# Local attention: the scores of even and odd heads on eight small tiles of TensorE and in two PSUM banks, the turned weights in the bank of the turned queries and keys

## The chip, the cores and the metric

One core of a Trainium2 chip runs the whole program. The metric is the time of one execution on the device, in microseconds; three runs of the kernel before are shown, and one more execution was profiled. PE is TensorE, ACT ScalarE, DVE VectorE, POOL GpSimd, SP SyncE.

## What is computed

The input x is [8, 512, 128]. After a layer norm, two branches are added to it: a causal attention (16 heads of 8) and a six-layer local transformer with 16 heads of 64 and windows of 32 tokens. The change is in the local attention of the six layers, cut here to what matters (`look` puts the window before in front of each window, so that 32 queries see 64 keys):

```python
x = attn_layer(shift_tokens(x), Wqkv[i], q_scale[i], k_scale[i], Wo[i]) + x      # six times, each with an ffn_layer after it
q, k, v = split(x @ Wqkv)                       # 16 heads of 64
q, k = l2norm(q) * qs, l2norm(k) * ksc          # then rotated by position
bq = q.reshape(b, h, nw, 32, 64); bk2, bv2 = look(k), look(v)     # [b, h, nw, 64, 64]
sim = einsum('bhwie,bhwje->bhwij', bq, bk2) * 8
attn = softmax(where(mask, -max, sim), -1)
out = einsum('bhwij,bhwje->bhwie', attn, bv2) @ Wo
```

All of it is float32.

## The kernel before, in words

**Work and order.** The tokens of a layer are 32 tiles of 128 (8 batches of 4). `pipeline` (L240) is a software pipeline over tiles that PE, ACT, DVE and POOL each write out by hand in the same `step`: step t handles tile t with lag 0, the tile before it with lag 1, and so on up to lag 6. A step has a first half (`wp` = 0) and a second half (`wp` = 1). The engines run their instructions strictly in the order written and meet only through semaphores. The first 6 steps of a layer fill the pipeline, the middle ones are a loop of four steps a pass, the last ones drain it. The six layers are 192 tiles.

**A tile's way.** The 1024 queries and 1024 keys of a token come in four chunks `c` of 512 (0 and 1 are the queries, 2 and 3 the keys).
- PE `project(c)` (L587) writes chunk c into one of two banks with three matmuls of 512 columns.
- ACT `square(c)` (L933) squares it. DVE `rotate(c)` (L1227, the multiplication at L1236) multiplies it by the rotation and frees the bank. POOL `add(c)` (L1505) adds the halves.
- DVE sums the squares (L1246), ACT `norms` (L949, L952, L956) makes of them the inverse norms `rn`, POOL `scale` (L1519) multiplies the chunk by them.
- A tile later, PE `turn_qk(c)` (L602, transposes at L614) turns the chunk in four transposes into `rbank`, the one bank for this, and ACT `turned_qk(c)` (L959) copies it out: chunks 0 and 1 with two copies of 64 partitions each into `qbd`, chunks 2 and 3 with one into `kT`. The semaphore `ev` counts these copies, and the next `turn_qk` waits for it, because it writes the same bank. `windows` (PE L665, transposes at L673, ACT L1012, semaphore `xwev`) uses `rbank` too, once a step, between chunks 2 and 3.
- Two tiles later, PE `score(wp)` (L618) adds the scores of two of the four windows of a tile to a mask that ACT `mask_ahead` (L985) copied into `sbank` beforehand. `qbd` holds the queries of two heads in the two diagonal blocks of a 128 x 64 operand, the rest is zero: 16 matmuls of 128 rows, 64 columns and 64 moving columns give 8 pairs of heads for two windows. Each float32 matmul shows as two matmuls and two weight loads in the profile.
- DVE `shift(wp)` (L1249) takes the maximum of each row (L1256) and subtracts it (L1259, semaphore `sub`), ACT `exp` (L983), DVE `sums` (L1269, L1271), POOL `normalise` (L1527, semaphore `pn`).
- PE `turn_p(wp)` (L637, transposes at L645) turns the weights into a bank of their own, `tbank`. ACT `turned_p` (L993) copies them out into `pT` (semaphore `ptev`). PE `weigh` (L649) multiplies them with the tokens of the windows, ACT `weighed` (L1002) copies the result into `ysb`.
- PE `project_out` (L677) multiplies four of the 16 heads by `wvo` in each half of most steps; DVE adds the sum to x.

**The order of one step.** On PE, in each half: turn_qk(2wp), project(2wp), project(2wp+1), turn_p(wp), in the second half windows, then weigh, score(wp), turn_qk(2wp+1), project_out (L702 to L712). On ACT, in each half: mask_ahead, turned_qk(2wp), square(2wp), square(2wp+1), exp, norms, in the second half windows, then turned_p, weighed, in the first half heads_of_tokens, and turned_qk(2wp+1) (L1022 to L1035). On DVE: rotate, rotate, sums, shift, square_sums (L1300 to L1305). On POOL: add(2wp), in the second half load_next (L1475, L1477), scale, scale, normalise, add(2wp+1), in the first half rests_of_tile (L1484) (L1531 to L1540).

All matmuls are recorded at L401, all plain copies of ACT at L790.

## Time and profile before

| | |
|---|---|
| runs | 3914.37, 3914.64, 3911.06 us; median 3914.37 us |
| the profiled execution | 3916.98 us |
| its span, from the first to the last instruction | 3915.2 us |
| its mean granted TensorE clock | 0.960 |
| busy: PE, ACT, DVE, POOL | 3617.0, 3010.4, 2778.3, 2730.6 us |

How it is read: by busy time PE leads, with 92% of the span, before ACT (77%), DVE (71%) and POOL (70%). A matmul's end is modelled in the profile, so starts are read for PE rather than ends. The time between two starts on one engine is what an instruction costs it; where an instruction starts a few hundredths of a microsecond after another engine's instruction has ended, it waited for that.

### The profile page before, as it was taken

The numbers are of one execution on the slowest core, as the hardware profiler recorded it, in microseconds if no ns is written. First come the engines' busy times: TensorE is split into PE (matmuls) and PEld (weight loads), VectorE is DVE, ScalarE is ACT, GpSimd is POOL, SyncE is SP. The second block draws the span as 40 slices with busy tenths as digits, with TensorE's granted clock in tenths as the row PEclk, the third lists the DMA queues.
The fourth block names the chain that finished last, engine by engine and source line by source line (L and its number), as shares of the span: only waits on it lengthen the run. The fifth ranks groups of instructions, "written<-read, shape, count | busy, mean of one in ns | idle before, by whom it ended". The sixth has DMA issues, their size and how long they took to land.

```text
span 3915.2 us, 94663 instructions
## 1 busy us (share of the span) xinstructions
PE 3617.0 (92%) x30894; PEld 2685.2 (69%) x30894; DVE 2778.3 (71%) x3770; ACT 3010.4 (77%) x6096; POOL 2730.6 (70%) x2889
## 2 busy tenths in 40 slices
PE   6898689999889999899999899999799999799998
PEld 3444367777667777677777677777577776577776
DVE  4566377776677776677776677776677776677776
ACT  3555478888688887688887688886688886788885
POOL 3454378886388884588884688883688882788872
PEclk7999789999999999899999899999899999899999
DMA  4223200000100000000001000001000001000002
GB/s 132 85 90 92 56 1 1 0 0 1 30 2 1 0 0 22 9 2 0 0 0 29 2 2 0 0 0 29 2 2 0 0 0 29 2 1 0 0 1 71
DMA packets 59745, 67.76 MB, mean 17 GB/s; under 512 B 12006, under 2 KB 40164, under 8 KB 58468
## 3 DMA queue, kind: packets, MB, share of 16 engines
q1 hardware_dynamic: 59492, 64.64, 5.8%
q8 instruction: 128, 2.10, 0.2%
q14 instruction: 125, 1.02, 0.1%
HBM read 46.27 MB, written 18.35 MB: 17 GB/s over the span
## 4 chain that ended last, share of the span: by engine, by line
POOL 41%; issue 29%; PE 19%; ACT 5%; DVE 3%; POOLq 2%; DMA 1%; SPq 1%; ACTq 0%; DVEq 0%
PE bank L401 16%; POOL sb_area L1505 16%; POOL sb_area L1519 12%; POOL sb_area L1527 6%; POOL sb_xs L1477 2%; POOL sb_xs L1475 2%; POOL sb_xwin L1484 2%; PE bank L614 2%; ACT sb_area L790 1%; DVE sb_area L1157 1%; ACT sb_area L940 1%; ACT sb_area L983 1%; DMA sb_wqk_lo<-qk_rows 1%; ACT sb_area L842 0%; ACT sb_lnb L952 0%
## 5 line engine op out<-in xcount | busy, mean ns | idle before, releaser
L790 ACT ACTIVATE sb_area<-bank 128x512 f32<-128x512 f32 (+4 forms) x2149 | 1315.2, 648 | 266.2 <-PE bank L614 206.4
L1236 DVE TENSOR_TENSOR sb_area<-bank,sb_rots 128x1024 f32<-128x1024 f32 x768 | 907.4, 1220 | 625.6 <-ACT sb_area L940 619.0
L1505 POOL TENSOR_TENSOR sb_area<-sb_area 128x512 f32<-128x512 f32 x768 | 983.6, 1281 | 311.8 <-DVE sb_area L1236 311.3
L401 PE MATMUL bank<-sb_area 128*64 128x64 f32 (+6 forms) x17104 | 1053.9, 276 | 10.2 <-DMA sb_area<-in_c_crot 3.5
L401 PEld LDWEIGHTS bank<-sb_area 128*64 128x64 f32 (+4 forms) x17104 | 750.0, 146 | 280.8 <-issue 244.0
L1519 POOL TENSOR_TENSOR sb_area<-sb_area,sb_rn 128x512 f32<-128x512 f32 x768 | 785.0, 1043 | 49.9 <-POOL sb_xs L1477 40.8
L401 PE MATMUL bank<-sb_area,sb_wvo 128*128 128x256 f32 x3072 | 728.3, 381 | 3.1 <-DVE sb_xT L1291 3.1
L401 PE MATMUL bank<-sb_wqk_hi,sb_xwin 128*128 128x512 f32 x1536 | 606.6, 436 | 43.0 <-POOL sb_xwin L1484 38.4
L614 PE MATMUL bank<-sb_ident,sb_area 128*128 128x128 f32 x3072 | 507.3, 288 | 134.1 <-POOL sb_area L1519 90.0
L401 PEld LDWEIGHTS bank<-sb_area,sb_wvo 128*128 128x128 f32 x3072 | 555.0, 190 | 75.2 <-issue 8.8
L614 PEld LDWEIGHTS bank<-sb_ident,sb_area 128*128 128x128 f32 x3072 | 330.9, 143 | 304.4 <-POOL sb_area L1519 211.7
L940 ACT ACTIVATE sb_area<-bank 128x512 f32<-128x512 f32 x768 | 439.2, 597 | 82.8 <-PE bank L401 42.7
L1246 DVE TENSOR_REDUCE sb_ssq<-sb_area 128x16 f32<-128x1024 f32 x384 | 464.1, 1209 | 0.0
L1527 POOL TENSOR_TENSOR sb_area<-sb_area,sb_srec 128x512 f32<-128x512 f32 x384 | 401.2, 1045 | 81.1 <-DVE sb_srec L1271 81.1
L401 PE MATMUL bank<-sb_wqk_lo,sb_xwin 128*128 128x512 f32 (+4 forms) x1280 | 423.0, 414 | 29.7 <-POOL sb_xwin L1412 13.8
L401 PEld LDWEIGHTS bank<-sb_wqk_hi,sb_xwin 128*128 128x128 f32 x1536 | 303.3, 197 | 109.0 <-issue 43.4
L790 ACT ACTIVATE bank<-sb_lmask 128x512 f32<-128x512 bf16 x384 | 231.0, 601 | 100.7 <-DVE sb_area L1259 95.1
L1269 DVE TENSOR_REDUCE sb_ssum<-sb_area 128x8 f32<-128x512 f32 x384 | 260.0, 677 | 45.6 <-ACT sb_area L983 45.6
L1259 DVE TENSOR_TENSOR sb_area<-bank,sb_smax 128x512 f32<-128x512 f32 x384 | 265.6, 692 | 13.1
L1256 DVE TENSOR_REDUCE sb_smax<-bank 128x8 f32<-128x512 f32 x384 | 253.0, 659 | 24.8 <-PE bank L401 24.5
L401 PEld LDWEIGHTS bank<-sb_wqk_lo,sb_xwin 128*128 128x128 f32 (+1 forms) x1280 | 206.4, 200 | 88.5 <-issue 26.8
L1157 DVE TENSOR_REDUCE sb_area<-bank 128x2 f32<-128x1024 f32 (+3 forms) x256 | 203.6, 823 | 88.6 <-PE bank L401 87.1
(116 smaller groups left out, 4107.3 us busy)
## 6 DMA issues: line engine op xcount, KB each, us to landing
qk_rows<-sb_p SPq DMA_DIRECT2D x52, 256.0 KB, 4.2
sb_wqk_hi<-qk_rows SPq DMA_DIRECT2D x32, 256.0 KB, 2.9
sb_wqk_lo<-qk_rows SPq DMA_DIRECT2D x32, 256.0 KB, 2.7
sb_area<-in_Wqkv SPq DMA_DIRECT2D x7, 1024.0 KB, 5.7
sb_area<-in_WvT SPq DMA_DIRECT2D x7, 512.0 KB, 7.5
sb_wo_bd<-in_Wo SPq DMA_DIRECT2D x14, 256.0 KB, 8.5
sb_area<-in_x SPq DMA_DIRECT2D x4, 512.0 KB, 6.0
sb_area<-in_x SPq DMA_DIRECT2D x8, 256.0 KB, 2.9
```

The lines of the kernel that those rows point to most:

```text
L401: return nc.tensor.matmul(o, a, b, start=start, stop=stop, skip_group_check=True)
L614: m = nc.tensor.transpose(rbank[:, j * P:(j + 1) * P], qn[:, c, j * P:(j + 1) * P], ident[:, :])
L790: return nc.scalar.activation(o, i, ACT.Copy)
L940: nc.scalar.activation(sqb[:, c, :], pj[c % 2][:, :], ACT.Square).then_inc(S["sq"], 1)
L1236: tt_(t12[:, c % 2, :, :].rearrange("p u (h d) -> p u h d", h=8), src, bc(rots[:, tt, s, :, :], [P, 2, 8, D], 2), ALU.mult).then_inc(S["ro ...
L1246: nc.vector.tensor_reduce(ssq[:, tt % 2, half, :], sqb[:, 2 * half:2 * half + 2, :].rearrange("p c (h d) -> p (c h) d", h=8), AX.X, ALU.add)\
L1256: nc.vector.tensor_reduce(smax[:, wp, :], s3, AX.X, ALU.max).then_inc(S["smax"], 1)
L1259: tt_(dd[:, wp, :].rearrange("p (h k) -> p h k", h=HP), s3, bc(smax[:, wp, :], [P, HP, 64], 2), ALU.subtract).then_inc(S["sub"], 1)
L1269: nc.vector.tensor_reduce(ssum[:, wp, :], d3, AX.X, ALU.add).then_inc(S["ssum"], 1)
L1505: pt_(qn[:, c, :].rearrange("p (h e d) -> p h e d", h=8, e=2), t12[:, c % 2, 0, :].rearrange("p (h e d) -> p h e d", h=8, e=2), swapped, A ...
L1519: pt_(sums_of_heads, sums_of_heads, r, ALU.mult).then_inc(S["qn"], 1)
L1527: pt_(dd[:, wp, :].rearrange("p (h k) -> p h k", h=HP), dd[:, wp, :].rearrange("p (h k) -> p h k", h=HP), srec[:, wp, :].unsqueeze(2).to_b ...
```

## The change

The scores of a head go on a tile of TensorE of their own: 64 rows (even heads on partitions 0 to 63, odd heads on 64 to 127) by 32 columns (the 32 queries of a window), and the even heads' scores go to one bank, the odd ones' to another. `qbd` is read without its zero blocks. 16 matmuls of 128 rows by 64 columns become 32 of 64 rows by 32 columns, each over 64 moving columns, ordered so that eight in a row use eight different tiles. The second bank is what was `tbank`; `turn_p` now uses `rbank`, between turn_qk(2wp) or windows and turn_qk(2wp+1), with the waits that this needs. `windows` moves ahead of project(3) on PE and ahead of square(3) on ACT; on ACT `turned_p` moves ahead of `norms`. The waits of `score` become a function of their own, `masked_and_turned`, which is called before `weigh`. Masking, maximum and subtraction read or write the two banks as [128, 2, 256]. The order of heads changes with it, and `project_out` takes the blocks of `wvo` in the new order.

```diff
-        pj, rbank, sbank, tbank, ybank, mbank = ps[0:2], ps[2], ps[3], ps[4], ps[5:7], ps[7]
+        pj, rbank, ybank, mbank = ps[0:2], ps[2], ps[5:7], ps[7]
+        sbanks = banks[:, 3:5, 0:256]
...
                     # turn_qk
+                        if c % 2 == 1 and (w := behind(t, i, part, 3)):
+                            pe.wait_ge(S["ptev"], g_of(w[1]) * 8 + 2 * w[0] + c // 2 + 1)
...
-                    def score(wp):
+                    def masked_and_turned(wp):
+
                         if not (v := behind(t, i, part, 2)):
                             return
                         tt, bt = v
                         pe.wait_ge(S["ev"], g_of(bt) * 16 + 4 * tt + 4)
                         if part == 0 and t == 2 and wp == 0:
                             pe.wait_ge(S["sub"], g_of(bt) * 8)
-                            mm(sbank[:, :], identb[:, :], lmask[:, 0, :], True, False)
+                            pe.wait_ge(S["ptev"], g_of(bt) * 8)
+                            for h2 in range(2):
+                                mm(sbanks[:, h2, :], identb[:, :], lmask[:, 0, 256 * h2:256 * h2 + 256], True, False)
                         else:
                             pe.wait_ge(S["masked"], g_of(bt) * 8 + 2 * tt + wp)
-                        for g in range(HP):
-                            for x in range(2):
-                                hp, w = 2 * (g // 2) + x, wp + 2 * (g % 2)
-                                k0 = tt * P + w * WIN
-                                m = mm(sbank[64 * x:64 * x + 64, g * 64:(g + 1) * 64],
-                                       qbd[:, tt % 2, hp, w, :, :].rearrange("p a b -> p (a b)"),
-                                       kT[:, hp, k0:k0 + 2 * WIN], False, x == 1 and g == HP - 1)
+
+                    def score(wp):
+                        if not (v := behind(t, i, part, 2)):
+                            return
+                        tt, bt = v
+                        for i_ in range(2):
+                            for w in range(2):
+                                k0, c0 = tt * P + (wp + 2 * w) * WIN, (2 * i_ + w) * 64
+                                for j in range(4):
+                                    for h2 in range(2):
+                                        rows, hp = slice(64 * h2, 64 * h2 + 64), 4 * i_ + j
+                                        m = mm(sbanks[WIN * j:WIN * j + WIN, h2, c0:c0 + 64],
+                                               qbd[rows, tt % 2, hp, wp + 2 * w, h2, :], kT[rows, hp, k0:k0 + 2 * WIN],
+                                               False, i_ == 1 and w == 1)
                         m.then_inc(S["score"], 1)
...
                     # turn_p
                         pe.wait_ge(S["pn"], m_ + 2)
                         pe.wait_ge(S["ptev"], m_)
+                        if v := behind(t, i, part, 1):
+                            if wp == 0:
+                                pe.wait_ge(S["ev"], g_of(v[1]) * 16 + 4 * v[0] + 1)
+                            else:
+                                pe.wait_ge(S["xwev"], g_of(v[1]) * 4 + v[0] + 1)
+                        else:
+                            pe.wait_ge(S["ev"], (l + 1) * (16 * B))
                         for j in range(4):
-                            m = nc.tensor.transpose(tbank[:, j * P:(j + 1) * P], dd[:, wp, j * P:(j + 1) * P],
+                            m = nc.tensor.transpose(rbank[:, j * P:(j + 1) * P], dd[:, wp, j * P:(j + 1) * P],
                                                     ident[:, :])
...
                     # project_out
-                                m = mm(mbank[:, 0:256], wvo[:, h, :], ysb[:, hf, :, h * WIN:(h + 1) * WIN],
+                                m = mm(mbank[:, 0:256], wvo[:, 2 * (h % HP) + h // HP, :], ysb[:, hf, :, h * WIN:(h + 1) * WIN],
...
                         turn_qk(2 * wp)
                         project(2 * wp)
+                        if wp == 1:
+                            windows()
+                        weighing = behind(t, i, part, 4 - wp)
+                        if not weighing:
+                            masked_and_turned(wp)
                         project(2 * wp + 1)
                         turn_p(wp)
-                        if wp == 1:
-                            windows()
+                        if weighing:
+                            masked_and_turned(wp)
                         weigh(4 - wp, 1 - wp)
                         score(wp)
                         turn_qk(2 * wp + 1)
...
                     # ACT: mask_ahead, turned_p, and the order of a half
-                        copy(sbank[:, :], lmask[:, 0 if first else 1, :]).then_inc(S["masked"], 1)
+                        copy(sbanks, lmask[:, 0 if first else 1, :].rearrange("p (b n) -> p b n", b=2)).then_inc(S["masked"], 1)
...
-                        copy(pT[:, wp, :], tbank[:, :]).then_inc(S["ptev"], 1)
+                        copy(pT[:, wp, :], rbank[:, :]).then_inc(S["ptev"], 1)
...
                         square(2 * wp)
+                        if wp == 1:
+                            windows()
                         square(2 * wp + 1)
                         exp(3 - wp, 1 - wp)
+                        turned_p(wp)
                         norms(1 - wp, 1 - wp)
-                        if wp == 1:
-                            windows()
-                        turned_p(wp)
                         weighed(4 - wp, 1 - wp)
...
                     # DVE: shift
-                        s3 = sbank[:, :].rearrange("p (h k) -> p h k", h=HP)
-                        nc.vector.tensor_reduce(smax[:, wp, :], s3, AX.X, ALU.max).then_inc(S["smax"], 1)
+                        s3 = sbanks.rearrange("p b (h k) -> p b h k", h=4)
+                        nc.vector.tensor_reduce(smax[:, wp, :].rearrange("p (b h) -> p b h", b=2), s3, AX.X, ALU.max).then_inc(S["smax"], 1)
...
```

## Rows read from the trace of the kernel before

**Rows 1.** Busy time (instructions) of PE, PEld, DVE, ACT, POOL over one step.

```profile
1453.62:1468.01 14.39, 14.27 (x137) 11.07 (x135) 11.05 (x15) 12.62 (x27) 12.30 (x14) 1.00 0.00 0
```

**Rows 2.** Timeline of PE over that step: start, length in us, instructions.

```profile
1456.52 1.89 PE L401 MATMUL bank<-sb_area,sb_wvo 128*128 128x256 f32 x8
1458.48 0.65 PE L614 MATMUL bank<-sb_ident,sb_area 128*128 128x128 f32 x4
...
1460.48 0.66 PE L645 MATMUL bank<-sb_ident,sb_area 128*128 128x128 f32 x4
1461.07 2.22 PE L401 MATMUL bank<-sb_area 64*128 64x256 f32 x40
1463.21 0.66 PE L614 MATMUL bank<-sb_ident,sb_area 128*128 128x128 f32 x4
1463.71 1.89 PE L401 MATMUL bank<-sb_area,sb_wvo 128*128 128x256 f32 x8
1465.65 0.63 PE L614 MATMUL bank<-sb_ident,sb_area 128*128 128x128 f32 x4
...
1466.59 0.63 PE L401 MATMUL bank<-sb_wqk_hi,sb_xwin 128*128 128x512 f32 x2
...
1467.53 0.60 PE L645 MATMUL bank<-sb_ident,sb_area 128*128 128x128 f32 x4
1467.96 0.38 PE L673 MATMUL bank<-sb_ident,sb_xs 128*128 128x128 f32 x2
```

**Rows 3.** Timeline of ACT over that step.

```profile
1455.02 0.21 ACT L956 ACTIVATE sb_rn<-sb_lnb 128x16 f32<-128x16 f32 x1
...
1459.17 1.20 ACT L790 ACTIVATE sb_area<-bank 64x512 f32<-64x512 f32 x2 [0.81 <-PE bank L614]
1460.39 1.08 ACT L940 ACTIVATE sb_area<-bank 128x512 f32<-128x512 f32 x2
1461.36 0.63 ACT L983 ACTIVATE sb_area<-sb_area 128x512 f32<-128x512 f32 x1
...
1462.73 1.51 ACT L790 ACTIVATE sb_area<-bank 128x512 f32<-128x512 f32 x2
...
1464.32 1.19 ACT L790 ACTIVATE sb_area<-bank 64x512 f32<-64x512 f32 x2
1465.53 0.60 ACT L790 ACTIVATE bank<-sb_lmask 128x512 f32<-128x512 bf16 x1
1466.32 0.60 ACT L790 ACTIVATE sb_area<-bank 128x512 f32<-128x512 f32 x1 [0.19 <-PE bank L614]
1467.02 1.30 ACT L940 ACTIVATE sb_area<-bank 128x512 f32<-128x512 f32 x2
```

**Rows 4.** Groups by shape, whole trace: busy us, mean ns of one, idle us before.

```profile
L401 PE MATMUL bank<-sb_area,sb_wvo 128*128 128x256 f32 x3072 | 728.3, 381 | 3.1 <-DVE sb_xT L1291 3.1
...
L401 PEld LDWEIGHTS bank<-sb_area 128*64 128x64 f32 x12288 | 392.1, 138 | 125.4 <-issue 125.4
```

**Rows 5.** Timeline of DVE over that step, one row.

```profile
1467.65 2.36 DVE L1236 TENSOR_TENSOR sb_area<-bank,sb_rots 128x1024 f32<-128x1024 f32 x2 [1.03 <-ACT sb_area L940]
```

**Rows 6.** Timeline of POOL over that step.

```profile
1457.38 2.04 POOL L1519 TENSOR_TENSOR sb_area<-sb_area,sb_rn 128x512 f32<-128x512 f32 x2 [0.23 <-POOL sb_xs L1477]
1459.38 1.04 POOL L1527 TENSOR_TENSOR sb_area<-sb_area,sb_srec 128x512 f32<-128x512 f32 x1
...
1468.96 1.28 POOL L1505 TENSOR_TENSOR sb_area<-sb_area 128x512 f32<-128x512 f32 x1 [0.69 <-DVE sb_area L1236]
```

**Rows 7.** Timeline of the weight loads: the scores of one half, later in the layer.

```profile
1505.12 1.01 PEld L401 LDWEIGHTS bank<-sb_area 128*64 128x64 f32 x32 [0.33 <-issue]
```

**Rows 8.** Timeline of PE in the causal branch: matmuls on four column tiles of 32.

```profile
301.91 0.82 PE L401 MATMUL bank<-sb_area 128*32 128x256 f32 x16
```

**Rows 9.** Timeline where the pipeline drains: the first half without project.

```profile
1516.23 1.20 ACT L790 ACTIVATE sb_area<-bank 64x512 f32<-64x512 f32 x2 [0.52 <-PE bank L614]
1516.24 0.42 PEld L645 LDWEIGHTS bank<-sb_ident,sb_area 128*128 128x128 f32 x4 [0.29 <-POOL sb_area L1527]
```

More of the change, by code:

```diff
@@ L1254, in shift @@
                         dve.wait_ge(S["score"], m_ + 3)
-                        s3 = sbank[:, :].rearrange("p (h k) -> p h k", h=HP)
-                        nc.vector.tensor_reduce(smax[:, wp, :], s3, AX.X, ALU.max).then_inc(S["smax"], 1)
+                        s3 = sbanks.rearrange("p b (h k) -> p b h k", h=4)
+                        nc.vector.tensor_reduce(smax[:, wp, :].rearrange("p (b h) -> p b h", b=2), s3, AX.X, ALU.max).then_inc(S["smax"], 1)
                         dve.wait_ge(S["smax"], m_ + 1)
                         dve.wait_ge(S["pt"], m_ + 1)
-                        tt_(dd[:, wp, :].rearrange("p (h k) -> p h k", h=HP), s3,
-                            bc(smax[:, wp, :], [P, HP, 64], 2), ALU.subtract).then_inc(S["sub"], 1)
+                        tt_(dd[:, wp, :].rearrange("p (b h k) -> p b h k", b=2, h=4), s3,
+                            bc(smax[:, wp, :].rearrange("p (b h) -> p b h", b=2), [P, 2, 4, 64], 3), ALU.subtract).then_inc(S["sub"], 1)
                     def sums(lag, wp):
```

## The prediction

> **What bounds the kernel now.** I read the busy times first, then the windows view of one step in the middle of a layer, then the timelines of that step engine by engine. Over the span PE is busy for 92%, which makes the scores look like the right place to save. The step agrees: it lasts 14.39 us and PE is busy for 14.27 of them, ACT for 12.62, POOL for 12.30, DVE for 11.05 [rows 1]. All four are so full that the bound has to be sought in the hand-overs: who starts within a few hundredths of a microsecond after whom.
>
> Start at turn_qk(0), 1458.48, the transposes of the first query chunk. ACT copies it out from 1459.17, and from there to 1465.51 ACT never pauses: two copies, two squares, exp, norms, turned_p, weighed, a split of tokens, and the two copies of chunk 1 (1464.32 plus 1.19) [rows 2, 3]. Those last copies free rbank, and PE's turn_qk(2) starts at 1465.65, 0.14 after them. PE itself would have been ready earlier: project_out started at 1463.71 and is eight matmuls of 0.216 (1.89 less the last one's own 0.38, over seven), so it was through at 1465.44 [rows 2, 4]. Here PE waits 0.21 for ACT. Then project(2) and turned_qk(2) lead to square(2) at 1467.02 [rows 3], rotate(2) on DVE follows at 1467.65 [rows 5], add(2) on POOL at 1468.96 [rows 6]. A step earlier POOL's scale of chunk 0 began at 1457.38, and one of its two operations (1.02) later, at 1458.40, PE could start turn_qk(0): again PE was ready sooner, at 1456.52 + 1.73 = 1458.25 [rows 2, 6].
>
> The ring closes: 0.69 (turn_qk(0) to ACT) + 6.34 (ACT's run) + 0.14 + 1.37 (turn_qk(2) to square(2)) + 0.63 + 1.31 + 2.81 (add(2) to the next scale, 1457.38 + 14.39) + 1.10 (to the next turn_qk(0)) = 14.39. No score and no weigh lies on it. PE is nearly full, but it waits for ACT in the first half (0.21) and for POOL in the second (0.23).
>
> **The change, part by part.** Steps are counted as 31 intervals of 14.39 in each of 6 layers, 186 in all.
>
> *The scores.* Now 32 passes (16 matmuls, two passes each) load in 1.01 us [rows 7]; less the last load's own 0.14 [rows 4] that is 0.058 for each of 16 rounds of two passes on the two column tiles (0.87 over 15 gaps), 0.92 in all. The change makes 64 passes, eight tiles at a time. That tiles side by side do overlap is shown for four column tiles: 16 passes, eight of 256 and eight of 128 columns, take 0.82 us including the last one's latency [rows 8]; one after another, at the 0.216 that 256 columns cost project_out and half of it for 128, they would take 2.6. Weigh does the same with two row tiles. If eight overlap as well, there are eight rounds of 0.058, 0.46 in all: 0.46 saved in each half. The bounds: nothing shown forbids a round shorter than 0.058, but the 64 moving columns are the same, so 0.46 is the best; the worst is the density of passes that the scores have now, 0.029 apart, 64 of them in 1.86. I take 0.46, since the row of four tiles is nearest.
>
> The Trainium skill speaks against this: "TensorE: Matmul & The Clock Gate", section "Wait — 56ns, not 53.3ns?", says that start-to-start never drops below about 25 ns however few columns a matmul has. By it the 64 passes would take an estimated 1.6 us, and the sum would be that of the slow rival below. The densest long row of this trace, 0.029, would agree with such a floor, while the 16 passes on four tiles don't test it, since they average 0.04 or more.
>
> *What the saving reaches.* In the first half PE would be through at 1464.98 instead of 1465.44, and still wait for ACT's copies until 1465.65. The saving is hidden by ACT's run: nothing.
>
> *ACT's order.* turned_p before norms: the same instructions, so the same 6.34. turned_p(0) needs the transposes of turn_p(0), which now wait for the copies of chunk 0 (end 1460.37, plus 0.14: 1460.51, against 1460.48 now, set by POOL's normalise) [rows 2, 3, 6]. They end by 1461.2, exp only at 1461.99. Nothing. turn_qk(1) waits for ptev (about 1462.5) and started at 1463.21 [rows 2]. Nothing.
>
> *The second half.* windows now waits for chunk 2's copy (1466.32 + 0.60), so it starts at 1467.06, and project(3) behind it at 1467.28; without it it was at 1466.82 (the second of the two passes that begin at 1466.59, 0.63 less a pass's own length of about 0.40) [rows 2]. Square(3) moves by the same 0.46, from 1467.73 to about 1468.2 (the second of the two squares, 1467.02 + 1.30 - 0.60). ACT copies windows at about 1467.6 to 1468.0, so turn_p(1) starts at 1468.08 instead of 1467.53. By the distances of the first half, weigh follows 0.59 later (1468.67), and project_out is through 4.37 after weigh: 1473.04 at today's scores, 1472.58 with the faster ones. turn_qk(0) is due at 1472.87 by POOL. So the faster scores are needed here to hide the new order, and leave 0.29. On ACT this half has room: it idles 0.81 before turned_qk(0) [rows 3]. rn of chunk 0 is ready at 1455.23 and used at 1457.38 [rows 3, 6]; it comes about 1.1 later. Nothing.
>
> *Masked_and_turned.* Its waits stand ahead of weigh now. The mask of score(1) is written from 1465.53 to 1466.13 [rows 3], long before PE comes there; the one of score(0) likewise before ACT's run. Nothing; if that cover were gone, weigh and all behind it would slip.
>
> *Mask, maximum, subtraction over two banks, wvo in another order, two mask matmuls for one.* The same elements. No row shows two strided banks for the mask; between nothing and the 0.19 that ACT idles behind the mask [rows 3] it costs nothing.
>
> *Filling and draining.* In the first drain step there is no project to cover the shared bank: turn_p(0), at 1516.24 now, must wait until 1516.23 + 1.20 + 0.14 = 1517.57 [rows 9], and in the second half windows and turn_p(1) follow one another through ACT. Walking through it, the second weigh of that step moves by about 1.75. From there PE is the bound, and three scores give back 0.46 each: +0.4 a layer, +2 in all. The bounds are all of the gain and none of the cost (-8) and the reverse (+11).
>
> **Sum.** 3916.98 + 0 + 2 = 3919 for the profiled execution, which was 2.6 over the median of the runs: 3917. A measurement of this kernel can tell about 0.2% (8 us) from no change, so this is no change. This case's own range is 3906 to 3927.
>
> **The rivals.**
> 1. *PE is the bound after all (faster).* For it: 14.27 of 14.39 busy [rows 1]. Each step would lose 2 x 0.46 and gain 0.33 (turn_p(1) is 0.55 late, less the two windows transposes that no longer stand behind it, 0.11 each by the lengths of four and of two [rows 2]): -0.59, times 186 is -110, so 3807. Against it: the two waits of 0.21 and 0.23. A part of it, -10 to -60, comes if the reordered ACT run is shorter by 0.05 to 0.3. Chance 0.20.
> 2. *The scores do not overlap between row tiles (a little slower).* They keep 0.92, and the second half of PE then ends 0.17 after POOL: 186 x 0.17 = +32, so 3949. It decides once scores take over 0.75 us. Chance 0.14, with small mishaps of the shared bank (a wait of ACT or PE that I put too early) in it.
> 3. *Passes cannot start closer than 0.029 (much slower).* PE becomes the bound in both halves: the first loses 0.93 - 0.21 = 0.72, the second 0.93 + 0.17 = 1.10, 1.82 x 186 = +339, so 4256. Against it stands that PE's sequencer and queue are nowhere seen to lag behind a long matmul; for it, that nothing denser lasts anywhere here. Chance 0.13. With the floor of the Trainium skill ("TensorE: Matmul & The Clock Gate") in place of 0.029 it would be an estimated 4160.
> 4. *The change does not do what it says*, the tiles being taken as full ones, is the second or third rival by its time.
>
> **How the numbers follow.** No change 0.53, faster 0.20, slower 0.27 (0.14 + 0.13). The likeliest case gives 3917. The range leaves out the third rival and the far end of the first: 3850 to 3960. The chances of over 0.2% either way are those of the cases, since the likeliest lies within it.
>
> **What would show it.** If right: steps between the transposes of windows still 14.39; 64 weight loads of a half's scores in about 0.6 us; ACT without a pause from turned_qk(0) to the copies of chunk 1, turn_qk(2) 0.14 behind them; PE idle about 0.7 before turn_qk(2); project(3) about 0.45 later after project(2) than now. Wrong: a step other than 14.39. Under 14.2, ACT's run is not what holds it; over 14.5, look whether project_out ends against turn_qk(0) (second rival) or the 64 loads take over 1.5 us (third).

## The result, and the profile after

The changed kernel takes 4027.33 us (median of 4 runs, 4023.62 to 4033.70) against 3913.19 for the kernel before (4 runs, 3911.06 to 3914.64): a ratio of 1.0298, 95% interval 1.0282 to 1.0314. It is 3% slower, 114 us. The forecast was 3917, and the range ended at 3960.

The changed lines have new numbers: turn_qk is L616 (L614 before), turn_p L664 (L645), the transposes of windows L692 (L673), mm L402 (L401), the copies L814 (L790), the loop of the pipeline L244 (L243). The page, parts 1 to 3:

```profile
span 4021.9 us, 119551 instructions
PE 3576.8 (89%) x43188; PEld 2550.0 (63%) x43188; DVE 2780.0 (69%) x3770; ACT 3020.5 (75%) x6096; POOL 2731.5 (68%) x2889
q8 instruction: 434, 7.11, 0.8%
```

PE is busy for 40 us less than before, and the span is 107 us longer (the two profiled executions took 3916.98 and 4023.62 us; the medians above are 114 apart). So the time did not go into work on PE. The third row is a queue that the prediction never looked at, the one that brings instructions to the engines: 434 packets of 16 KB, where the kernel before has this:

```profile
q8 instruction: 128, 2.10, 0.2%
```

**A step in the middle of the loop** is what was forecast. Windows view (length, then busy time and instructions of PE, PEld, DVE, ACT, POOL, then the granted clock as a share of full speed, the share of DMA and its GB/s), timelines of the weight loads, of PE, of POOL and of ACT:

```profile
1486.50:1500.86 14.36, 14.03 (x199) 10.23 (x199) 11.04 (x15) 12.66 (x26) 12.30 (x14) 1.00 0.01 2
```

```profile
1490.15 0.70 PEld L402 LDWEIGHTS bank<-sb_area 64*32 64x32 f32 x64 [0.33 <-issue]
1493.63 0.42 PEld L616 LDWEIGHTS bank<-sb_ident,sb_area 128*128 128x128 f32 x4 [0.70 <-POOL sb_area L1543]
```

```profile
1489.09 1.92 PE L402 MATMUL bank<-sb_area 64*128 64x256 f32 x72
1490.94 0.66 PE L616 MATMUL bank<-sb_ident,sb_area 128*128 128x128 f32 x4
1491.43 1.89 PE L402 MATMUL bank<-sb_area,sb_wvo 128*128 128x256 f32 x8
1493.66 0.63 PE L616 MATMUL bank<-sb_ident,sb_area 128*128 128x128 f32 x4 [0.33 <-POOL sb_area L1543]
...
1494.98 0.44 PE L692 MATMUL bank<-sb_ident,sb_xs 128*128 128x128 f32 x2
...
1496.06 0.63 PE L664 MATMUL bank<-sb_ident,sb_area 128*128 128x128 f32 x4
1496.62 1.92 PE L402 MATMUL bank<-sb_area 64*128 64x256 f32 x72
```

```profile
1491.59 2.04 POOL L1543 TENSOR_TENSOR sb_area<-sb_area,sb_rn 128x512 f32<-128x512 f32 x2
```

```profile
1487.19 1.20 ACT L814 ACTIVATE sb_area<-bank 64x512 f32<-64x512 f32 x2 [0.80 <-PE bank L616]
...
1492.33 1.18 ACT L814 ACTIVATE sb_area<-bank 64x512 f32<-64x512 f32 x2
1493.55 0.60 ACT L814 ACTIVATE bank<-sb_lmask 128x512 f32<-128x512 bf16 x1
```

The step takes 14.36 (14.39 in [rows 1]). ACT runs without a pause from 1487.19 to 1493.51, 6.32 us (6.34 forecast); turn_qk(2) starts 0.15 behind it (0.14). The releaser printed in its row is POOL's L1543, but the one of its two operations that counts had ended a microsecond earlier (it began at 1491.59 and took 1.02); what comes last is ACT's copy, as the prediction's ring says. (The second operation ends at 1493.63, just ahead of the transposes; that they do not wait for it shows in heads_later below.) Counted from turn_qk(2), windows comes 1.32 later (forecast 1.41), turn_p(1) 2.40 (2.43), weigh 2.96 (3.02). The scores saved less than I took: from weigh to turn_qk(1) it is 1.85 us now and 2.14 before (1461.07 to 1463.21, [rows 2]), so 0.29 and not 0.46 for each half.

**The turn of the loop** is where the time is. The pipeline's loop runs four steps a pass and has five back edges and one exit in each of six layers. The row of TensorE's sequencer (PEldq) for the branch at the loop's end: count, least, median and longest duration in ns, first and last start.

```profile
L244 PEldq COMPARE_BRANCH  x36: 83/4640/5150, 614.5 to 3869.9; - x36
```

and of the kernel before:

```profile
L243 PEldq COMPARE_BRANCH  x36: 83/215/248, 627.3 to 3763.9; - x36
```

The branch that went back in 0.215 us takes 4.64. In the timeline of PE around the second layer's first back edge (the branch begins at 1205.1):

```profile
1205.25 1.89 PE L402 MATMUL bank<-sb_area,sb_wvo 128*128 128x256 f32 x8
1210.12 0.65 PE L616 MATMUL bank<-sb_ident,sb_area 128*128 128x128 f32 x4 [2.98 <-issue]
```

project_out, which was already in PE's queue, covers the first two microseconds; then PE has nothing for 2.98, and no engine is named as the releaser, only "issue", which is time in which the engine waited for nothing that the profile shows. The list of waits has it as one row (us in total, times, longest), 30 times, which is six layers by five back edges:

```profile
PE bank L616 <- issue: 88.6, 30, 3.5
```

From windows to windows across a back edge it is 18.28 us on average, across the exit 14.67; in the kernel before they are 14.70 and 14.65. That is 30 x 3.58 = 107 us.

On q8 the stretch from 1203 to 1213 us has

```profile
q8 instruction: 3, 0.05, 3.0%
```

Two of the three packets start within 1.1 us of the branch's start, the third at 1210.5, and the others of the pass follow one by one, 4 to 12 us apart. The trace has nine of them in every pass that begins with a slow branch.

### The profile page after: what moved, and what is told of

Its sections match the earlier page's. It is cut to its first block, busy times and chain, and to the rows that moved or that the text cites. A ratio compares the mean times of both kernels' runs of the same rounds, so it can differ in the third digit from the quotient of the medians.

```text
span 4021.9 us, 119551 instructions
## 1 busy us (share of the span) xinstructions
PE 3576.8 (89%) x43188; PEld 2550.0 (63%) x43188; DVE 2780.0 (69%) x3770; ACT 3020.5 (75%) x6096; POOL 2731.5 (68%) x2889
## 3 DMA queue, kind: packets, MB, share of 16 engines
q14 instruction: 125, 1.02, 0.1%
## 4 chain that ended last, share of the span: by engine, by line
POOL 40%; issue 30%; PE 21%; ACT 4%; DVE 2%; POOLq 2%; DMA 1%; SPq 0%; ACTq 0%; DVEq 0%
PE bank L402 17%; POOL sb_area L1529 15%; POOL sb_area L1543 12%; POOL sb_area L1551 6%; PE bank L616 2%; POOL sb_xs L1501 2%; POOL sb_xs L1499 2%; POOL sb_xwin L1508 2%; ACT sb_area L814 1%; DVE sb_area L1181 1%; PE bank L664 1%; ACT sb_area L866 0%; DMA sb_wqk_lo<-qk_rows 0%; ACT sb_wqk_hi L814 0%; ACT sb_area L1007 0%
## 5 line engine op out<-in xcount | busy, mean ns | idle before, releaser
L814 ACT ACTIVATE sb_area<-bank 128x512 f32<-128x512 f32 (+4 forms) x2149 | 1374.2, 648 | 374.6 <-PE bank L616 302.7
L402 PE MATMUL bank<-sb_area 64*32 64x64 f32 (+5 forms) x29392 | 937.9, 253 | 10.4 <-DMA sb_area<-in_c_crot 3.7
L1543 POOL TENSOR_TENSOR sb_area<-sb_area,sb_rn 128x512 f32<-128x512 f32 x768 | 785.3, 1044 | 64.0 <-POOL sb_xs L1501 39.5
L402 PEld LDWEIGHTS bank<-sb_area 64*32 64x32 f32 (+4 forms) x29392 | 627.8, 115 | 280.9 <-issue 243.1
L616 PE MATMUL bank<-sb_ident,sb_area 128*128 128x128 f32 x3072 | 514.5, 292 | 257.5 <-POOL sb_area L1543 150.1
L402 PE MATMUL bank<-sb_area,sb_wvo 128*128 128x256 f32 x3072 | 728.3, 381 | 3.1 <-DVE sb_xT L1315 3.1
L402 PE MATMUL bank<-sb_wqk_hi,sb_xwin 128*128 128x512 f32 x1536 | 671.4, 458 | 43.6 <-POOL sb_xwin L1508 38.6
L616 PEld LDWEIGHTS bank<-sb_ident,sb_area 128*128 128x128 f32 x3072 | 336.9, 144 | 434.6 <-POOL sb_area L1543 254.1
L402 PEld LDWEIGHTS bank<-sb_area,sb_wvo 128*128 128x128 f32 x3072 | 555.0, 190 | 75.5 <-issue 8.8
L402 PE MATMUL bank<-sb_wqk_lo,sb_xwin 128*128 128x512 f32 (+4 forms) x1280 | 425.8, 413 | 28.9 <-POOL sb_xwin L1436 14.2
L402 PEld LDWEIGHTS bank<-sb_wqk_hi,sb_xwin 128*128 128x128 f32 x1536 | 316.1, 206 | 103.6 <-issue 44.0
L814 ACT ACTIVATE bank<-sb_lmask 128x512 f32<-128x512 bf16 x384 | 230.6, 600 | 71.6 <-DVE sb_area L1283 65.6
L664 PE MATMUL bank<-sb_ident,sb_area 128*128 128x128 f32 x1536 | 247.7, 285 | 15.1 <-ACT sb_area L814 14.3
```

Of the source, the lines that this page charges most:

```text
L402: return nc.tensor.matmul(o, a, b, start=start, stop=stop, skip_group_check=True)
L616: m = nc.tensor.transpose(rbank[:, j * P:(j + 1) * P], qn[:, c, j * P:(j + 1) * P], ident[:, :])
L664: m = nc.tensor.transpose(rbank[:, j * P:(j + 1) * P], dd[:, wp, j * P:(j + 1) * P], ident[:, :])
L814: return nc.scalar.activation(o, i, ACT.Copy)
L1543: pt_(sums_of_heads, sums_of_heads, r, ALU.mult).then_inc(S["qn"], 1)
```

## The experiments

13 kernels ran. Two theories at the start. *Fetch*: the loop's body on TensorE grew by 512 score matmuls and their loads and no longer stays in what the engine keeps of its program, so that it is fetched anew at each back edge. *Order*: the new waits or the small tiles make the turn slow. A third, *ring*, is the prediction's own: ACT's run sets the step and the scores do not. "Body" below is where the loop's body begins and ends in TensorE's program, in instructions of 64 bytes; it is read from the compiled program and not from a trace. "Slow" is how many of the 30 back edges took 4.3 to 5.3 us rather than about 0.22, q8 is the count of 16 KB packets, and "step" is the length of a step in the middle, within 0.01. Each ratio is to the kernel before as timed beside that kernel (medians of 3908 to 3915), so a difference of two times of the table is good to some 5 us only.

| kernel | time, us | ratio to before [95%] | body | length | slow | q8 | step |
|---|---|---|---|---|---|---|---|
| before | 3913.19 | | 8264 to 9441 | 1177 | 0 | 128 | 14.39 |
| after | 4027.33 | 1.0298 [1.0282, 1.0314] | 8778 to 10472 | 1694 | 30 | 434 | 14.37 |
| old_scores_new_order | 3930.93 | 1.0049 [1.0032, 1.0066] | 8264 to 9446 | 1182 | 0 | 128 | 14.43 |
| scores16 | 3910.13 | 0.9997 [0.9986, 1.0008] | 8266 to 9448 | 1182 | 0 | 128 | 14.38 |
| scores24 | 3907.43 | one run | 8522 to 9960 | 1438 | 0 | 146 | 14.38 |
| grown_before | 4117.73 | one run | 8776 to 10465 | 1689 | 3 | 191 | 15.53 |
| heads_later | 3865.92 | 0.9884 [0.9861, 0.9906] | 8264 to 9441 | 1177 | 0 | 128 | 14.19 |
| after_heads_later | 3995.3 | one run | 8778 to 10472 | 1694 | 30 | 434 | 14.19 |
| trim1 | 3914.98 | 1.0008 [0.9995, 1.0020] | 8758 to 10437 | 1679 | 0 | 164 | 14.37 |
| trim1_heads_later | 3891.30 | 0.9935 [0.9916, 0.9954] | 8758 to 10437 | 1679 | 0 | 164 | 14.18 |
| trim2_heads_later | 3883.39 | 0.9921 [0.9896, 0.9945] | 8758 to 10432 | 1674 | 0 | 164 | 14.17 |
| padded16 | 3923.40 | 1.0022 [1.0004, 1.0040] | 8771 to 10458 | 1687 | 1 | 173 | 14.37 |
| padded1695 | 4029.78 | 1.0296 [1.0253, 1.0339] | 8782 to 10477 | 1695 | 30 | 434 | 14.37 |
| after_shift200 | 3922.52 | 1.0035 [1.0023, 1.0046] | 8978 to 10672 | 1694 | 0 | 170 | 14.37 |
| trim1_shift40 | 4030.14 | 1.0308 [1.0287, 1.0329] | 8798 to 10477 | 1679 | 30 | 434 | 14.37 |

### The change in two halves, and by size

**old_scores_new_order**: the changed order and the shared bank with the 16 old score matmuls a half. score(wp) and the bank of the scores are those of before, all else that of after.

```diff
-    for i_ in range(2):
-        for w in range(2):
-            ... 8 tiles of 64 x 32 ...
+    for g in range(HP):
+        for x in range(2):
+            ... one matmul of 128 x 64, as before ...
```

> The order, the waits and the shared bank of the changed kernel, with the 16 score matmuls, the one score bank and the mask of before. Fetch theory (the changed kernel loses its time at the back edge of PE's loop, whose body has grown from 1176 to 1693 recorded instructions a pass and is fetched anew in each pass: the branch takes 3.9 us on average instead of 0.2): the body is back at about 1180, no branch takes more than 0.3 us, and what is left is the drain (the last interval between the windows transposes of a layer 13.6 instead of 12.05, 6 x 1.6 = +9) and, in the middle, PE's second half, which has lost 0.29 of faster scores and had 0.17 to spare: steps of 14.49 instead of 14.37, +22. Together about 3945, between 3922 and 3955. Rival (the order and the shared bank are what costs): the time stays near 4027 or goes above it.

3930.93, 0.5% slower than before, with no slow branch. So the order of the waits and the shared bank are not what makes the turn slow; they cost 19 us by themselves (the kernel before took 3911.75 beside it). The faster scores then take back 16 of them (trim1, below).

**scores16** and **scores24** leave out half and a quarter of the new score matmuls:

```diff
     for w in range(2):
+        if w == 1:
+            continue
```

```diff
+        if i_ == 1 and w == 1:
+            continue
```

> The changed kernel without the scores of every second window of a half: 16 of the 32 score matmuls are left out, everything else stands. Its loop body has about as many PE instructions as that of before (1180). Fetch theory: branches of 0.2 us, steps of 14.37, the drain's 9 us remain: about 3920. Rival (tiles of 64 x 32 themselves, the second bank or the order cost it at the turn of a pass): branches stay above 3 us or the passes still begin with a step of over 17 us, about 4020.

> The changed kernel with 24 of the 32 score matmuls of a half (a quarter of the scores left out): about 1435 PE instructions a pass, half-way between before and after. Fetch theory: either it still fits (branch 0.2 us, about 3920) or it does not (branch 3 to 5 us, about 4020); not half of it, unless only the overflow is fetched, which would give branches of about 2 us. Rival: 4020 whatever the number.

Both have fast turns, as *fetch* expected, and the step is 14.37 or 14.38 with a half, three quarters or all of the score matmuls, as *ring* expected: the scores are not on the path of a step.

**grown_before** is the kernel before with a matmul of 8 columns behind each of its 16 score matmuls (its scores are partly counted twice). Its body is as long as that of after, in the old order and on the old tiles.

```diff
+    m = mm(sbank[64 * x:64 * x + 64, g * 64:g * 64 + 8], ..., kT[:, hp, k0:k0 + 8], False, ...)
```

> The kernel before, in its own order and banks, with each of its 16 score matmuls followed by a second one over 8 columns only (it adds those scores once more, so they are counted twice): as many PE instructions a pass as the changed kernel (1690). Fetch theory: branches of 4 to 5 us and nine instruction packets a pass although nothing of the change is in it; the steps grow too, since PE gets 32 short passes more a half (0.3 to 0.5 us): about 4100 to 4180 in all. Rival (order, banks or tiles): branches stay at 0.2 us.

```profile
L243 PEldq COMPARE_BRANCH  x36: 83/215/5301, 627.9 to 3959.2; - x36
```

Mostly a miss for fetch as I had put it: only three of its 30 back edges are slow, each with nine packets on q8. But those three are in a kernel with none of the change's waits or small tiles, so a slow branch needs neither. The step went from 14.39 to 15.53, with a row like this in each half:

```profile
1496.17 1.97 PEld L401 LDWEIGHTS bank<-sb_area 128*64 128x64 f32 x64 [0.33 <-issue]
```

64 loads of a half take 1.97 us instead of 1.01 for 32, 1.9 a step more, of which 1.14 shows. TensorE has room in this step, about 0.8 (1.9 less 1.14). The time of 4117.73 lies in the range that was expected, but by luck: the turns were forecast slow and were not, and the steps grew by more than forecast, 1.14 instead of 0.6 to 1.0.

### The ring

**heads_later** and **after_heads_later** move the copy of the next tile's heads (0.2 us of ACT's time) out of the long run into the second half, one tile earlier, and POOL's subtraction of the rests with it. All arithmetic stays.

```diff
-    if wp == 0 and not (part == 0 and t == 0) and (v := behind(t, i, part, -1)):
-        heads_of_tokens(*v)
     turned_qk(2 * wp + 1)
+    if wp == 1 and (v := behind(t, i, part, -2)):
+        heads_of_tokens(*v)
```

> The kernel before with the split of the tokens (heads_of_tokens on ACT, rests_of_tile on POOL) moved from the first half of a step to the end of its second half and done one tile earlier. It takes 0.2 us out of ACT's run between turn_qk(0) and the copies of chunk 1, and puts it where ACT idles 0.37 behind the mask. Ring theory (a step's 14.39 is the ring through ACT's first half, DVE, POOL and back): steps of 14.2, 186 x -0.2 = -37: about 3876; PE, with 0.21 to spare, is then as late as ACT. Rival (PE is the bound, busy for 99% of a step): no change, 3913. If POOL's second half, which gets 0.45, has less room than its 0.67 of idle time suggests, some of it is lost again.

> The same move in the changed kernel. Ring theory: steps of 14.37 - 0.2 = 14.17 or a little less, since PE has 0.5 to spare in its first half there, the loop's branches as slow as in the changed kernel: about 3990. Rival (PE bound): 4027.

0.2 us out of ACT's run takes 0.2 us off the step, 14.39 to 14.19 in the one kernel and 14.37 to 14.19 in the other; the time falls by 1.2% in the one and 32 us in the other (one run). The timeline of heads_later, ACT, then PE, then POOL:

```profile
1251.48 1.20 ACT L790 ACTIVATE sb_area<-bank 64x512 f32<-64x512 f32 x2 [0.81 <-PE bank L614]
...
1255.04 2.58 ACT L790 ACTIVATE sb_area<-bank 128x512 f32<-128x512 f32 x4
```

```profile
1257.77 0.63 PE L614 MATMUL bank<-sb_ident,sb_area 128*128 128x128 f32 x4
```

```profile
1255.88 2.04 POOL L1519 TENSOR_TENSOR sb_area<-sb_area,sb_rn 128x512 f32<-128x512 f32 x2
```

ACT's run is 1251.48 to 1257.62, 6.14 instead of 6.34, and turn_qk(2) follows it by 0.15 as before. POOL's second scale ends at 1257.92, after turn_qk(2) has begun, so the transposes do not wait for it. The move also takes 0.46 us out of POOL's first half, which is not what shortened the step: before, POOL stood idle for 0.69 ahead of add(2), waiting for DVE [rows 6]. The ring of the prediction is what sets the step. heads_later also beats both kernels.

### Does the turn go away alone?

**trim1** is the changed kernel less one wait of TensorE that another implies.

```diff
-    pe.wait_ge(S["sq"], g)
     pe.wait_ge(S["rotd"], g)
```

**trim2_heads_later** and **trim1_heads_later** add the move of heads_later; trim2_heads_later also drops two more implied waits in the loop.

> The changed kernel; of TensorE's waits in the loop one is left out that another implies: project() no longer waits for the square of the bank, only for its rotation, which itself comes after the square. The same arithmetic, and 15 instructions fewer in the body of TensorE's loop (1679 instead of 1694). Instruction-fetch theory (the body just outgrew what TensorE keeps, the one with 1689 was fetched anew on 3 of its back edges only): branches of 0.22 us instead of 4.7, turn-of-pass step 14.7, no or a few of the 16 KB packets, time 3913 to 3922 (steps 14.37, plus 1.6 us a layer in the drain). If instead the turn of the pass is slow because of the order of the waits or of the score tiles: turn of pass still 17 to 18 us and the time still 4020 to 4035. If the limit lies lower than 1679: as now, 4020 to 4035, and the kernel with 1674 tells no more.

> The changed kernel with three implied waits of TensorE left out (body 1674 instead of 1694) and with the move of heads_later (the copy of the next tile's heads and the subtraction of its rests at the end of the second half, one tile earlier). Fetch theory plus ring theory: step 14.19, turn-of-pass step 14.4, branches 0.22 us, time 3865 to 3878: the before kernel with the same move (3866) plus 1.6 us a layer for the drain, less whatever faster scores give. If the faster scores are worth something once ScalarE's run is shorter (TensorE then being nearer the bound): steps under 14.1 and a time under 3860. If the branches stay slow: 3990 to 4000, as in after_heads_later.

> As trim2_heads_later, with the body at 1679 instead of 1674 instructions. Fetch theory: if the edge is a hard one above 1679, the same time as trim2_heads_later within 5 us, 3865 to 3878; if it is soft, a few slow back edges (5 us each) more than in the shorter one. Rival: slow at every turn, 3990 to 4000.

```profile
L244 PEldq COMPARE_BRANCH  x36: 83/215/248, 618.2 to 3760.7; - x36
```

This row is trim1's. 15 instructions fewer, and 112 us are gone: 3914.98, ratio 1.0008 [0.9995, 1.0020]. That is the time the change would have had without its turns, and the forecast was 3917. Each of the 270 packets that q8 carries more in after than in trim1 (434 less 164) belongs to a slow back edge, nine to each of 30. With the move, 3883.39 and 3891.30 are slower than the 3865 to 3878 expected, and the steps, 14.17 and 14.18, are what heads_later has: the faster scores bring nothing there either, and heads_later remains the fastest. They are 17 and 25 us over it, and most of that lies in the filling and draining: by intervals between windows, the third to fifth of a layer are together 1.4 and 1.3 longer than in heads_later, the last is 1.5 longer, and the 31 together take 440.0 and 440.7 instead of 437.1, which is 17 and 21 us in six layers.

**padded16** and **padded1695** put waits that are long over in the place of the one left out, one or two in each project():

```diff
+    for name in ("const", "c_weights"):
+        pe.wait_ge(S[name], 1)
     pe.wait_ge(S["rotd"], g)
```

> trim1 (one implied wait of TensorE left out) with a wait put in its place in project() that is over since the start of the program (the constants' loads): the body of TensorE's loop is 1687 instructions instead of 1679; nothing else changes, and TensorE waits for nothing more. Size theory: between 1679 (never fetched anew) and 1694 (always); as in the kernel with 1689, at most the first back edge of a layer is slow (5 us each), so 3913 to 3945. If it was the wait on the square itself that made the turn slow: no slow branch at all, 3913 to 3920.

> trim1 with two such waits on semaphores that are long over: the body is 1695 instructions, one more than in the changed kernel, and TensorE still waits for nothing more than in trim1. Size theory: every back edge is fetched anew, branches 4.3 to 5.2 us, turn-of-pass step 17.7, time 4020 to 4035 as the changed kernel. If it was the wait on the square: branches 0.22 us and 3913 to 3922.

TensorE waits for nothing more than in trim1. With one wait one back edge of 30 is slow, with two all are (padded1695):

```profile
L244 PEldq COMPARE_BRANCH  x36: 83/4634/5017, 616.7 to 3873.9; - x36
```

So it was never the wait on the square: this rival is refuted, and what is left is how many instructions the body has or where they lie.

### Length or place?

In all runs so far a longer body also ended later. **after_shift200** is the changed kernel with 200 instructions ahead of the loop over the layers, executed once; **trim1_shift40** has 40 ahead of the short body.

```diff
+    for _ in range(400):      # 80 in trim1_shift40
+        pe.wait_ge(S["const"], 9 * 16)
     with pe.Fori(0, layers) as l:
```

> The changed kernel with 400 waits that are long over, 200 instructions, put before TensorE's loop over the layers; they run once. The loop's body stays at 1694 instructions and begins 200 instructions further on (at 8978 of the program instead of 8778, ending at 10672 instead of 10472). Length theory (a body over some 1690 is fetched anew on every pass): unchanged, branches 4.7 us, 4020 to 4035. Block theory (the packets are of 256 instructions; by the runs so far a boundary lies just under 10472, and so at about 8932 and 10724; the body touches eight blocks as it lies now, seven once it begins past 8932): branches of 0.22 us, turn-of-pass step 14.7 and 3910 to 3925, like trim1 plus at most 12 us for the 200 instructions once.

> trim1 (body of 1679 instructions, no slow branch) with 80 waits that are long over, 40 instructions, before the loop over the layers. The body begins at 8798 and ends at 10477, past the boundary that the block theory puts just under 10472. Length theory: as trim1, 3907 to 3925, branches 0.22 us. Block theory: every back edge slow, branches 4.3 to 5.2 us, time 4020 to 4035, with a body shorter than that of four kernels in which no or few back edges were slow.

after_shift200, then trim1_shift40:

```profile
L244 PEldq COMPARE_BRANCH  x36: 83/215/243, 630.1 to 3778.1; - x36
```

```profile
L244 PEldq COMPARE_BRANCH  x36: 83/4663/5173, 617.1 to 3873.0; - x36
```

Length alone falls. The same body of 1694 instructions is slow at 30 back edges where it begins at 8778 and at none where it begins at 8978; the body of 1679 is fast at 8758 and slow at 8798. The 200 instructions have a small price of their own: 3922.52 is 0.35% over the kernel before, trim1 0.08%.

What fits all the runs is a count of blocks. With 16 KB packets of 256 instructions and a boundary between 10465 and 10472, the boundaries are near 8676, 8932, ..., 10468, 10724. Every kernel with 30 slow back edges begins before 8932 and ends behind 10468 and so touches eight blocks; every other touches seven or fewer. Length still counts in that a body of 1177 or 1438 cannot touch eight wherever it lies. The two with one and three slow ones end 10 and 3 instructions short of the boundary. Seven blocks stay; with eight the pass costs nine packets, the eight of the body and, it seems, one ahead. That last reading, and that a body close under the boundary sometimes loses its first blocks to the one fetched ahead, is an inference from the counts; no run shows which block is dropped, and the place of the boundaries is itself worked out from which kernels were slow.

The Trainium skill, "Runtime: NRT & Kernel Launch", section "Instruction fetch mechanics", gives TensorE an instruction memory of 2048 instructions, refilled in blocks of 16 KiB, which are 256 instructions. By that figure it has room for an estimated eight blocks: seven of the body and one ahead fit, eight and one ahead do not. The packets of 16 KB agree, and so do seven blocks kept and eight not. The same section of the Trainium skill says that a taken branch whose target is outside "the current 2-page window" waits until the target has been fetched. The wait is there, 4.3 to 5.3 us for a back edge that fetches; the window of two is not what TensorE shows: in trim1 the target is 1679 instructions back, more than six blocks, and the branch takes 0.215 us with no packet on q8 between two back edges.

## Why the prediction was wrong

**The step that failed** is one that the sum does not have. "The scores. [...] The change makes 64 passes, eight tiles at a time" counts matmuls and costs their time in the array; 512 more instructions a pass of the loop (16 more matmuls, as two passes with a load each, in eight halves) were costed at nothing, and no term says so. "Steps are counted as 31 intervals of 14.39 in each of 6 layers" takes the 30 steps that cross a back edge for steps like the others; they measured 18.28 instead of the 14.70 of before, which is 107 us. The trace of before could have warned: 30 back edges of about 0.215 us and 128 packets of q8 in the whole span show a loop whose body, 1177 instructions, stays. That it would not stay at 1694 no row of before shows, but the turn of the loop was a place to state a bound for. The prediction's signs of being wrong would not have found it either: they all look at a step in the middle, and that step came as forecast.

**The sum without it was right.** trim1, which differs by one wait in each project(), takes 3914.98 against 3917 forecast, and 1.0008 of before. Its terms, one by one:

- *The ring sets the step*: right, 14.37 against 14.39, and heads_later moves it by what it takes out of ACT's run, 0.20.
- *The scores*: mis-sized. Not 0.46 but 0.29 saved a half. The passes are 0.0094 apart (the loads' 0.70 less a load's own 0.105, over 63 gaps), a round of eight 0.075 and not 0.058. It did no harm, since the gain is hidden in the first half and only covers the new order in the second: without it (old_scores_new_order) the step is 14.43 and the kernel 0.5% slower. That is the case of the prediction's second rival at half its price: 16 us over trim1, where the rival had 32.
- *The third rival*, passes no closer than 0.029, is refuted by the loads' 0.0094. (The starts of the matmuls themselves, by their records in the trace, are 0.010 apart: 1490.154 to 1490.796 over 63 gaps.) The Trainium skill, "TensorE: Matmul & The Clock Gate", section "Wait — 56ns, not 53.3ns?", gives about 25 ns as the least distance between starts. By the 0.010 here that does not hold for matmuls on different tiles.
- *The second half*: the offsets forecast for windows, turn_p and weigh were right within 0.09.
- *Filling and draining*: too small, but within its bounds of -8 to +11. The prediction walked through the draining alone and put the filling at nothing. Rows of rotate (shortest, median, longest in ns, then the first start and the last), before and trim1:

```profile
L1236 DVE TENSOR_TENSOR sb_area<-bank,sb_rots x768: 1214/1224/1227, 492.4 to 3791.0; 128x1024 f32<-128x1024 f32 x192
```

```profile
L1259 DVE TENSOR_TENSOR sb_area<-bank,sb_rots x768: 1211/1224/1227, 483.5 to 3787.4; 128x1024 f32<-128x1024 f32 x192
```

The stretch is 3298.6 in the one and 3303.9 in the other, +5.3 where I had +2. By intervals between windows the last of a layer is 13.61 instead of 12.05 and the third to fifth together 1.3 longer, the 31 together 446.3 instead of 444.1, while what lies outside them is 1.4 a layer shorter.

**The account of after.** The same row there:

```profile
L1260 DVE TENSOR_TENSOR sb_area<-bank,sb_rots x768: 1211/1224/1227, 478.1 to 3896.5; 128x1024 f32<-128x1024 f32 x192
```

3418.4, 119.8 more than before: 107 at the back edges, 5.3 as in trim1, and 7 more. Of these, against trim1, about 3 lie within the 31 intervals of the layers and about 3 between one layer's intervals and the next's (125.0 instead of 124.4, five times); what causes them stays open. The span is only 106.7 longer because the first rotate came 14.3 earlier. That is not the change: over the profiled runs it comes at 478 to 492 with the same code ahead of it, early and late with and without it.

**The range** left out only the third rival on the slow side, and what came was none of the rivals. That the time lies between the second and the third says nothing for either. PE's waits were all sought between engines; the one that came is between the engine and its own program.

## What to carry to other kernels

A loop's body has a size on each engine, and a change that splits TensorE's matmuls into many small ones pays in instructions: count them for a pass of the loop, look at the branch's duration and at the packets of the instruction queue, and state a bound for the turn. Where a wait reads "issue" once per pass and the branch takes microseconds, move the loop by some hundred instructions, or drop waits that others imply, before judging the change by its time. And what sets a step is best tested by taking a known piece out of the run that is thought to set it: 0.2 us less there was worth 1.2%, while scores faster by 0.29 a half were worth nothing but the cover of the new order.

## What the runs showed of the hardware that I had not expected

- TensorE keeps seven blocks of 256 instructions across a back edge and not eight; a back edge then takes 4.3 to 5.3 us instead of about 0.22, with nine packets of 16 KB. At a length close under that, the place decides: 40 instructions ahead of a loop cost 3%, and 200 ahead of another gave 2.6% back.
- Eight tiles of 64 x 32 take the 64 loads of 64 passes of 64 columns in 0.70 us, 0.0094 apart. A round of eight so takes 0.075, more than the 0.058 of a round of two on tiles of 128 x 64.
- Most of a slow branch shows in the time, not all: of one of 4.67 us PE was idle for 2.98, since its queue still held project_out's eight matmuls, and a step that crosses a back edge grew by 3.58.
